# A mixture-of-experts loop on one core: block counts read inside the pass and summed in registers, half of the row fill moved under attention, three raw weight buffers

## The reference, cut to what matters

```python
C = max(1, int(N * K * CAP_FACTOR / E))        # 234 rows an expert; N = 1250, K = 6, E = 64
topk_p, topk_i = jax.lax.top_k(router_probs, K)
...
expert_in = jnp.zeros((E, C + 1, D), x.dtype).at[se, safe_slot].set(x_flat[st])
...
hg = jnp.einsum('ecd,efd->ecf', expert_in, w_gate)
hu = jnp.einsum('ecd,efd->ecf', expert_in, w_up)
expert_out = jnp.einsum('ecf,edf->ecd', jax.nn.silu(hg) * hu, w_down)
...
sparse = jax.ops.segment_sum(fg[:, None] * expert_out.reshape(-1, D), dst, num_segments=N + 1)[:N]
```

## Time and profile before

| | us |
|---|---|
| median of three runs | 2476.49 (2473.33 to 2477.33) |
| the profiled execution, its own time | 2477.46 |
| its span, first to last instruction | 2475.8 |
| time outside the span | 1.66 |
| the expert loop, 722 to 1322 us | 600 |

### The profile page before, as it was taken

How to read it: one execution, slowest core, us unless ns; L and a number is a source line. 1 busy time by engine, 2 the same in 40 slices (tenths; PEclk the granted TensorE clock), 3 DMA queues, 4 the chain that set the end, 5 groups by cost and what they waited for, 6 DMA issues and landing times. The chain is left out here.

```text
span 2475.8 us, 36374 instructions
## 1 busy us (share of the span) xinstructions
PE 2052.7 (83%) x10667; PEld 1516.1 (61%) x10667; DVE 1339.6 (54%) x1905; ACT 1094.9 (44%) x1732; POOL 648.1 (26%) x469
## 2 busy tenths in 40 slices
PE   5765799778948888887875777999999994899998
PEld 2444544355536666666664745999845553799998
DVE  6555277434236655656561043555511217999997
ACT  2443466121025555555551013777601114766665
POOL 3000200001753333333334705787600004000000
PEclk8887899878979999999998888999999997999999
DMA  2391341112037766767763615887620003000000
GB/s 94 126 409 75 83 91 24 36 55 93 2 109 237 247 204 221 257 229 240 242 216 102 170 58 144 204 203 205 156 102 0 1 0 153 1 1 1 0 0 42
DMA packets 122528, 299.34 MB, mean 121 GB/s; under 512 B 51264, under 2 KB 58426, under 8 KB 112638
## 3 DMA queue, kind: packets, MB, share of 16 engines
q1 hardware_dynamic: 58686, 222.81, 26.5%
q0 software_dynamic: 63680, 74.56, 11.4%
HBM read 242.05 MB, written 70.67 MB: 126 GB/s over the span
## 5 line engine op out<-in xcount | busy, mean ns | idle before, releaser
L1911 PE MATMUL ps<-ft,kw 128*128 128x125 f32 x2880 | 343.2, 279 | 36.8 <-DVE ft L1836 23.7
L1911 PEld LDWEIGHTS ps<-ft,kw 128*128 128x128 f32 x2880 | 331.2, 193 | 51.0 <-DVE ft L1836 30.6
L1095 POOL DMA_INDIRECT xg<-nrows,idx x128 | 211.4, 1652 | 371.3 <-PE ps L1121 346.2
L1405 POOL DMA_INDIRECT pg<-prows,srcI x170 | 215.3, 1266 | 54.4 <-issue 39.2
L1179 ACT ACTIVATE wh<-wexp 128x2048 fp32r<-128x2048 f32 x64 | 122.7, 1918 | 169.3 <-DMA wexp<-wexp_d 76.9
L1134 PE MATMUL ps<-wh,xh 128*128 128x512 f32 x364 | 156.9, 431 | 42.9 <-issue 36.5
L1236 DVE TENSOR_TENSOR wl<-wexp,wh 128x2048 fp32r<-128x2048 f32 x64 | 146.8, 2293 | 73.5 <-issue 71.5
L1436 PEld LDWEIGHTS ps<-ehot,msg 125*128 125x128 f32 x1360 | 159.8, 193 | 11.7 <-issue 5.7
L1436 PE MATMUL ps<-ehot,msg 125*128 125x125 f32 x1360 | 160.5, 277 | 7.0 <-ACT ehot L1528 5.8
L1860 ACT ACTIVATE ksq<-ksrc,kn 128x750 f32<-128x750 f32 (+2 forms) x144 | 116.5, 813 | 97.9 <-DVE cube L1819 97.9
L1780 POOL COPY ksrc<-nT 128x500 f32<-128x500 f32 (+1 forms) x10 | 10.7, 1074 | 521.1 <-SPq L1771 281.3
(11 more groups left out here) (275 smaller groups left out, 4099.8 us busy)
## 6 DMA issues: line engine op xcount, KB each, us to landing
wexp<-wexp_d SPq DMA_DIRECT2D x64, 1024.0 KB, 5.2
yrows<-nought SPq DMA_DIRECT2D x1, 32768.0 KB, 84.8
wexp<-wexp_d SPq DMA_DIRECT2D x64, 512.0 KB, 5.7
yrows<-y SPq DMA_DIRECT2D x91, 256.0 KB, 3.5
attr<-attr_d SPq DMA_DIRECT2D x42, 250.0 KB, 5.1
kw<-kw_d SPq DMA_DIRECT2D x2, 4608.0 KB, 19.1
qs<-qk SPq DMA_DIRECT2D x32, 156.2 KB, 5.6
ks<-qk SPq DMA_DIRECT2D x32, 156.2 KB, 5.9
```

The costliest lines, as they stand in the source:

```text
L1095: pool.indirect_dma_start(xg[:, e % 2, h, :], None, d["nrows"], bass.IndirectOffsetOnAxis(ap=idx[:, 2 * e + h:2 * e + h + 1], axis=0), bou ...
L1405: pool.indirect_dma_start(pg[:, p % 4, t % 2, :], None, d["prows"], bass.IndirectOffsetOnAxis(ap=c.srcI[:, t:t + 1], axis=0)).then_inc(s_g ...
L1911: mm = pe.matmul(out[:, m * B:m * B + B], w[:, k, f, m * P:m * P + P], ft[:, f % RF, a:a + B], start=False, stop=False, skip_group_check=True)
```

## The change

It does four things.

- `expert_chunks` is replaced by a class `Passage`. The block count of expert e + 1 is loaded inside the passes of expert e (`fetch(e + 1)`, once a pass): on PE between the down product and the transposes of `he`, on ACT between `xh` and `y`, on DVE between `xl` and `hl`, and on SP behind the stores of an expert. The blocks before are no longer read but kept in registers (`total`, `add`): one sum on PE, DVE and SP, three on ACT.
- The raw ring `wexp` gets three slots (WR = 3). `routing` therefore loads three experts ahead instead of two, and SP's loads in the loop are for expert e + 4 where they were for e + 3, behind the same waits.
- `wl` is taken apart: `gl`, the rest of gate and up, is a ring of two (WG = 2), `dl`, the rest of down, a ring of three.
- The fill covers only the second row of each expert (h = 1), 16 MB. POOL zeroes a tile of 128x512 at the start of the scores' block, ahead of its four additions, and issues the transfer itself behind them. The old tile, SP's transfer and SP's waits in the first block are gone.

```diff
-WR, WS = 2, 3
+WR, WS, WG = 3, 3, 2
...
-                pool.memset(nought[:, :], 0.0).then_inc(s_nought, 1)
                 pool.memset(table[:, :, :], 0.0).then_inc(s_zero, 1)
...
-                sp.dma_start(every, nought[:, :].rearrange("p (o n) -> p o n", o=1).broadcast_to([P, CH * D // 1024, 1024]))\
-                    .then_inc(s_rows, 16)
...
+                pool.memset(nought[:, :], 0.0).then_inc(s_nought, 1)
                 for k in range(KD):
                     pool.tensor_tensor(c.xT[:, k, :], c.xT[:, k, :], c.nT[:, k, :], ALU.add).then_inc(s_res, 1)
+                pool.wait_ge(s_nought, 1)
+                second = d["yrows"][0:DUMP, :].rearrange("(p e h) f -> p e h f", p=P, h=2)[:, :, 1, :]
+                pool.dma_start(second, nought[:, :].rearrange("p (o n) -> p o n", o=1).broadcast_to([P, NE, D]))\
+                    .then_inc(s_rows, 16)
+                pool.wait_ge(s_rows, 16)
...
+class Passage:
+    def __init__(self, c, eng, name):
+        self.c, self.eng = c, eng
+        self.counts = [eng.alloc_register(name + "now"), eng.alloc_register(name + "next")]
+        self.sums = {}
+        self.fetch(0)
+    def fetch(self, e):
+        if e < NE:
+            count = self.eng.value_load(self.c.etab[0:1, 0, e:e + 1], min_val=1, max_val=2)
+            self.eng.reg_mov(self.counts[e % 2], self.eng.to_reg(count))
...
+    def add(self, name, e):
+        self.eng.reg_mov(self.sums[name], self.eng.to_reg(self.sum(name, 0, 2 * NE) + self.count(e)))
...
                 for e in range(NE):
-                    count, first = expert_chunks(c, pe, e)
                     pe.wait_ge(s_dlo, e + 1)
-                    with pe.Fori(0, count) as k:
+                    first = pas.sum("pen", e, 2 * e)
+                    with pe.Fori(0, pas.count(e)) as k:
                         n = first + k
                         gate_up(e, n)
                         down(bass.ds(pe.snap(used, min_val=0, max_val=WS - 1), 1), n)
+                        pas.fetch(e + 1)
                         pe.wait_ge(s_he, n + 1)
...
                     q = e % 2
-                    count, n = expert_chunks(c, act, e)
-                    mine = act.value_load(c.etab[0:1, 2, e:e + 1], min_val=min(e, 2) // 2, max_val=NE)
...
                     dve.wait_ge(s_ghi, e + 1)
-                    dve.tensor_tensor(wl[:, s, GU], wexp[:, r, GU], wh[:, s, GU].bitcast(F32), ALU.subtract)\
+                    dve.tensor_tensor(gl[:, e % WG, :], wexp[:, r, GU], wh[:, s, GU].bitcast(F32), ALU.subtract)\
                         .then_inc(s_glo, 1)
```

More of the change, by code:

```diff
@@ L595, in attention @@
         raw = sm("raw", [P, 2, N], F32)
+        nought = sm("nought", [P, D], F32)
+        s_nought, s_rows = c.sem("at_nought"), c.sem("at_rows")
         s_sc, s_ex, s_wt, s_av, s_raw, s_res = (c.sem("at_" + n) for n in ("sc", "ex", "wt", "av", "raw", "res"))
@@ L1004, in _, with count, total, sum @@
                                              ALU.mult, ALU.add).then_inc(s_x, 1)
-def expert_chunks(c, eng, e):
-    count = eng.value_load(c.etab[0:1, 0, e:e + 1], min_val=1, max_val=2)
-    before = eng.value_load(c.etab[0:1, 1, e:e + 1], min_val=0, max_val=2 * NE)
-    return count, before
+class Passage:
[8 more added lines that the diff above has]
+            self.eng.reg_mov(self.counts[e % 2], self.eng.to_reg(count))
+    def count(self, e):
+        return self.eng.snap(self.counts[e % 2], min_val=1, max_val=2)
+    def total(self, name):
+        self.sums[name] = self.eng.alloc_register(name)
+        self.eng.reg_mov(self.sums[name], 0)
+    def sum(self, name, low, high):
+        return self.eng.snap(self.sums[name], min_val=low, max_val=high)
+    def add(self, name, e):
+        self.eng.reg_mov(self.sums[name], self.eng.to_reg(self.sum(name, 0, 2 * NE) + self.count(e)))
 def experts(c, d, wexp, s_rgu, s_rdn):
@@ L1022, in experts @@
         xg = sb("xg", [CH, 2, 2, D], F32)
-        wh, wl = (sb("w" + n, [P, WS, WEXP], F32R) for n in "hl")
+        wh = sb("wh", [P, WS, WEXP], F32R)
+        gl, dl = sb("wgl", [P, WG, WGU], F32R), sb("wdl", [P, WS, WEXP - WGU], F32R)
         xh, xl = (sb("x" + n, [P, KD, CH], F32R) for n in "hl")
@@ L1052, in _ @@
                     .then_inc(s_tab, 16)
+                pas = Passage(c, sp, "sp")
+                pas.total("spn")
                 col = sp.alloc_register("ycol")
@@ L1068, in _ @@
                         sp.wait_ge(s_st[0], 16)
-                    count, n = expert_chunks(c, sp, e)
-                    with sp.Fori(0, count) as k:
+                    n = pas.sum("spn", e, 2 * e)
+                    with sp.Fori(0, pas.count(e)) as k:
                         sp.wait_ge(s_y, n + k + 2)
@@ L1075, in _ @@
                         sp.reg_mov(col, sp.to_reg(k + 2 * e))
+                    pas.add("spn", e)
+                    pas.fetch(e + 1)
                 ends = []
@@ L1081, in _ @@
                 to = sp.snap(col, min_val=0, max_val=P - 1)
-                sp.wait_ge(s_y, n + count + 2)
+                sp.wait_ge(s_y, pas.sum("spn", NE, 2 * NE) + 2)
                 sp.wait_ge(s_st[0], ends[0])
@@ L1143, in down @@
                         cols = slice(WGU + k * D, WGU + k * D + D)
-                        high, low = wh[:, slot, cols], wl[:, slot, cols]
+                        high, low = wh[:, slot, cols], dl[:, slot, k * D:k * D + D]
                         for i, (lhs, rhs) in enumerate(((hh, high), (hl, high), (hh, low))):
@@ L1166, in _ @@
                         turn(e + 2)
-                down((NE - 1) % WS, first + count)
+                    pas.add("pen", e)
+                down((NE - 1) % WS, pas.sum("pen", NE, 2 * NE))
             @block.scalar
@@ L1196, in _ @@
                         .then_inc(s_xh, 1)
+                pas = Passage(c, act, "act")
+                for name in ("actn", "act0", "act1"):
+                    pas.total(name)
                 for e in range(NE):
                     q = e % 2
-                    count, n = expert_chunks(c, act, e)
-                    mine = act.value_load(c.etab[0:1, 2, e:e + 1], min_val=min(e, 2) // 2, max_val=NE)
                     if e + 2 < NE:
@@ L1206, in _ @@
                     if e >= 2:
-                        act.wait_ge(s_st[q], mine * 16)
+                        act.wait_ge(s_st[q], pas.sum(f"act{q}", e // 2, e // 2 * 2) * 16)
+                    n, count = pas.sum("actn", e, 2 * e), pas.count(e)
                     with act.Fori(0, count) as k:
@@ L1219, in _ @@
                             .then_inc(s_hh, 1)
-                act.wait_ge(s_dn, n + count + 1)
+                    pas.add("actn", e)
+                    pas.add(f"act{q}", e)
+                act.wait_ge(s_dn, pas.sum("actn", NE, 2 * NE) + 1)
                 act.activation(ylast[:, :], c.ps[:, DOWN, :], ACT.Copy).then_inc(s_y, 1)
@@ L1242, in down_weights @@
                     dve.wait_ge(s_dhi, e + 1)
-                    dve.tensor_tensor(wl[:, s, DN], wexp[:, r, DN], wh[:, s, DN].bitcast(F32), ALU.subtract)\
+                    dve.tensor_tensor(dl[:, s, :], wexp[:, r, DN], wh[:, s, DN].bitcast(F32), ALU.subtract)\
                         .then_inc(s_dlo, 1)
@@ L1256, in _ @@
                     rest(j, c.psf[:, turned(0, j):turned(0, j) + 2 * CH])
+                pas = Passage(c, dve, "dve")
+                pas.total("dven")
                 for e in range(NE):
-                    count, n = expert_chunks(c, dve, e)
                     if e + 1 < NE:
@@ L1261, in _ @@
                         down_weights(e + 1)
+                    n, count = pas.sum("dven", e, 2 * e), pas.count(e)
                     with dve.Fori(0, count) as k:
@@ L1273, in _ @@
                             .then_inc(s_hl, 1)
+                    pas.add("dven", e)
     PS = 4
```

10 lines of the change are left out of this document (3 added, 7 removed).

## The result

| | us |
|---|---|
| before, measured with it | 2476.91 (2473.33 to 2478.73, 4 runs) |
| the changed kernel | 2375.66 (2373.47 to 2376.94, 4 runs) |
| ratio, 95% interval | 0.9592, 0.9575 to 0.9609 |
| its profiled execution | 2376.94, span 2375.2 |

The prediction said 2396, 2384 to 2434. The sign was right, and the time was missed by 20 us.

What follows compares the result with a forecast made beforehand. No engine is full; a chain between engines, headed by ACT's weight copy, bounds the expert loop. 81.6 + 1.2 - 3 + 1.0 - 0.5 = 80.3 us off 2477.46 gives 2397.2, median 2396; range 2384 to 2434.

Steps and rivals of the forecast that it cites:

- the sentence on the fill: First block: nobody waits for the old 32 MB transfer, so removing it gains nothing; POOL's earlier start gains 1.0 us.
- Its low end: Expert loop: DVE's and PE's gains count in full, 5.6 instead of 6.06 us in a third of one-pass experts, no late load.
- Heads and late loads: Expert loop: earlier register loads and a third raw slot cut 579.3 us to 497.7, a gain of 81.6 us.
- One-pass experts: Expert loop: each of the 37 one-pass experts would take 6.06 us.
- two-pass ones: Expert loop: each of the 25 two-pass experts would take 10.94 us.
- the ends: Expert 63's head, where no `turn` covers the loads: idle 1.40 us falls to 0.2, 1.2 us gained.
- The chain's head: Expert loop: ACT's weight copy stays the head of the chain, starting about 0.1 us after `turn` ends.
- Loads inside the passes: Expert loop: register loads moved into the passes are covered by other work and cost 0 us.
- Late loads: Expert loop: single weight loads no longer late; runs of one-pass experts may outrun the loading, 3 us set aside.
- rival A: Expert loop: DMA engines bind in one-pass experts, 7.44 us each, loop 51 us longer, 2444 us in all; 9%.
- Rival C: Scores' block: POOL's describing of the fill and DVE obstruct each other, 2465 us at 69 us, 2588 at 192; 5%.
- The zero fill ahead of POOL's additions: Scores' block: zeroing 512 columns ahead of POOL's additions costs 0.5 us, 0 to 1.0.

## Why the prediction missed

**The failed step** is the sentence on the fill: "The 32 MB themselves were issued at 113.37 and landed by 198.2, long before the scores' additions end at 295.3: nothing gained." I asked only who waits for the transfer, and nobody does. I did not ask what goes on beside it. It made DVE's register loads 0.70 us longer each (0.30 to 1.00) and so stretched ten rounds of a chain bound by DVE by 2.1 us each. The count by excess of a load holds at three sizes: two loads 1.27 (with the old fill back), three 2.08 (before), six 3.9 (doubled), so 0.64 to 0.69 a load. With the measured 18.7 us in that place of the sum the forecast would be 2396 - 17.7 = 2378, 3 us from the median. What could have been seen beforehand: the rows of the loads, 1.00 us in the flight and 0.30 behind it, and the gap of 2.94 ahead of L572 with a releaser that had begun 3.06 before. The rounds' periods alone would not have given the size: in the kernel before they are 6.2 to 7.2 outside the flight as well, for other reasons, where 5.6 to 5.9 is what the ten come to without it.

**The range.** Its low end had only the loop's engines gaining more than reckoned. (Its terms, 12 x 0.46 and the 3 us of late loads, give 2387 or 2388, not 2385; that changes nothing here.) No rival let the fill's removal be worth more than 1.0, so nothing reached below 2384.

**The other terms.**
- Heads and late loads: forecast 79.8 for `table` to `ylast`, measured 80.8. That it is right to 1 us is in part luck, since errors of a few us cancel inside it. One-pass experts were 0.05 shorter than forecast (37 x 0.05 = 1.9), two-pass ones 0.27 longer (25 x 0.27 = 6.8; 3 had been set aside), and the ends gave 4.1 instead of 1.2: 1.8 ahead of the first head, 2.3 behind the last.
- The chain's head: ACT's copy did stay it, at T + 0.1. What I did not ask is whether it had to wait for `turn` at all. The run without that wait says that 26 us more were there in the loop.
- Loads inside the passes at nothing: right in effect, on PE with room for one more, though PE's load is no longer the 0.30 us that it was at the heads: its median is 0.54 and its longest 1.00.
- Late loads: none is left, so rival A fell. The share of the DMA engines rose to 0.77 and the loads take 6.2 us to land, with one period more to do it.
- Rival C fell: the transfer's row on POOL is 2.99 us long, where I took 69, and DVE's additions up to its landing kept their 1.45. (POOL has nothing to do behind it but wait for the landing, so that the trace doesn't show whether it goes on describing.) The issue and the landing (57.1 us) on the timeline of POOL and the page's list of transfers, which answers to the earlier trace rows:

```profile
255.43 0.53 POOL L610 MEMSET nought<- 128x512 f32 x1 [225.33 <-POOLq L350]
263.41 11.18 POOL L612 TENSOR_TENSOR xT<-xT,nT 128x1250 f32<-128x1250 f32 x4 [7.46 <-issue]
274.55 2.99 POOL L615 DMA_DIRECT2D yrows<-nought  x1
```

```profile
yrows<-nought POOLq DMA_DIRECT2D x1, 16384.0 KB, 57.1
```

  The nearest row, a gather of 128 rows, taken 64 times, was the wrong measure. That error cost nothing in the sum, since the time lay free, but it carried rival C.
- The zero fill ahead of POOL's additions, 0.5: not to be told from the two lengths of that block.

## What to carry to other kernels

A transfer that nobody waits for can still be paid for: look at the work beside its flight before calling it hidden, and compare each kind of row inside and outside of it, those of the queues too, since the period of a loop can be long outside for another reason. Here the register loads were what showed it: count them in each bound chain, sum what can be summed, read the rest a round ahead, and put them behind work of the engine that is longer than they are. And when a chain's head has been found, ask what each of its waits is for, since the head may be there by a wait that one made earlier on the same engine has made needless.

## What the runs showed of the hardware that I had not expected

- A register load on DVE takes 0.30 us, and 1.00 while a transfer out of the core's memory moves 410 GB/s; with the register arithmetic behind it that is 0.70 and 1.37 of DVE's time (worked out from the doubled loads). While a transfer from device memory to device memory keeps the DMA engines as full (317 GB/s, share 1.00) it is 0.30 still. Whether the source or the rate does it stays open; a transfer out of the core's memory at a lower rate was not tried in that place. The loop of the changed kernel speaks for the source: PE's load mostly stands there 1.1 to 1.7 us behind the issue of a store of `y` out of the core's memory, and took 0.54 us in the median and up to 1.00; one at 742.9 took 0.88 while the DMA engines moved 165 GB/s. DVE's and ACT's loads in the same passes kept 0.31 and 0.28.
- DVE's instructions beside the same flight keep their length (`row` 2.70, `pairs` 1.50, `vs` 0.41). The Trainium skill, page "SBUF — State Buffer", section "Who interferes with whom", says that DMA never contends with a compute engine. For instructions on tiles the trace agrees. For DVE's reads of the same memory into registers it does not (0.30 and 1.00 us), and the measurement decides.
- A plain transfer of 8192 rows of 2 KB has a row of 2.99 us on POOL, as long as the longest gather of 128 rows (3.00), and lands after 57.1.
